# Two-block network on one Trainium2 core: the scores of parity 0 shifted by VectorE before one exponential, the steps of all queues reordered

## The reference

```python
xn = layernorm(x)
s = gru(xn)                      # a recurrence over 512 tokens, 256 hidden, as logs in the reference
g = silu(local_transformer(xn))  # 2 layers
x = x + s * g
xn = layernorm(x)
s = global_attention(xn)         # 16 heads over 512 tokens
g = silu(mixture_of_experts(xn)) # only the last item passes through the experts' real weights
x = x + s * g
```

```python
sim = einsum('bhwid,bhwjd->bhwij', bq, bk)
sim = where(mask, -finfo.max, sim)
attn = softmax(sim, axis=-1)
out = einsum('bhwij,bhwjd->bhwid', attn, bv)
```

## Time and profile before

| | us |
|---|---|
| median of 3 runs | 3660.54 (3658.41 to 3660.62) |
| profiled execution | 3663.09 |
| span of its instructions | 3661.3 |
| PE busy / DVE busy / ACT busy / POOL busy | 3026.1 / 2466.6 / 2551.7 / 922.2 |

### The profile page before, as it was taken

The page is one execution under the profiler, slowest core; times in us unless marked ns, Lnnn a source line. Parts: engine busy times, 40 slices in busy tenths (PEclk is TensorE's granted clock), DMA queues, the critical chain, the costliest instruction groups (busy, mean ns, idle before and its releaser), DMA issues.

```text
span 3661.3 us, 54935 instructions
## 1 busy us (share of the span) xinstructions
PE 3026.1 (83%) x20144; PEld 1454.9 (40%) x20144; DVE 2466.6 (67%) x4573; ACT 2551.7 (70%) x5722; POOL 922.2 (25%) x685
## 2 busy tenths in 40 slices
PE   4677897989888897979889897988889798988776
PEld 2343443434344343524344343534434343433242
DVE  3465867768685877768586776868586776857313
ACT  2466777868686777868677786868677786857444
POOL 1131323223131323313132322323132322312000
PEclk9889998999999999999999999999999998989887
DMA  2001010010101001010101001010101001011200
GB/s 71 3 1 51 18 51 17 14 58 19 58 14 51 21 31 41 14 58 18 54 18 51 21 25 47 14 58 19 54 18 47 21 14 55 19 51 36 83 9 16
DMA packets 113448, 122.78 MB, mean 34 GB/s; under 512 B 13426, under 2 KB 86684, under 8 KB 113180
## 3 DMA queue, kind: packets, MB, share of 16 engines
q1 hardware_dynamic: 113180, 119.26, 10.2%
HBM read 64.70 MB, written 54.53 MB: 33 GB/s over the span
## 4 chain that ended last, share of the span: by engine, by line
PE 45%; DVE 28%; ACT 19%; issue 5%; POOL 2%; SPq 1%; DMA 0%; DVEq 0%; POOLq 0%; ACTq 0%
PE pb L587 19%; PE o_bank L587 11%; PE s L587 6%; DVE nmax L1307 5%; PE e L587 5%; ACT ex L1033 5%; PE e L677 2%; DVE stat L1204 2%; ACT scratch L966 2%; DVE scratch L1213 2%; ACT mlp_h L990 1%; PE pb L731 1%; DVE scratch L1211 1%; DVE scratch L1245 1%; DVE stat L1233 1%
## 5 line engine op out<-in xcount | busy, mean ns | idle before, releaser
L1307 DVE TENSOR_REDUCE nmax<-s 128x1 f32<-128x512 f32 x1024 | 686.6, 684 | 404.1 <-PE s L587 398.3
L1033 ACT ACTIVATE ex<-s,nmax 128x512 f32<-128x512 f32 x1024 | 701.0, 686 | 253.0 <-DVE nmax L1307 218.9
L587 PE MATMUL o_bank<-ex,vsc 128*64 128x512 f32 x2048 | 542.0, 653 | 68.3 <-POOL vsc L1441 53.9
L587 PE MATMUL e<-wqkv,hsh 128*128 128x512 f32 x768 | 432.0, 645 | 85.4 <-ACT scratch L933 68.4
L1402 POOL TENSOR_TENSOR scratch<-scratch 128x1024 f32<-128x1024 f32 x128 | 304.6, 2379 | 768.8 <-DVE scratch L1214 599.7
L587 PE MATMUL s<-qs,ks 96*128 96x512 bf16 x1024 | 387.3, 404 | 121.1 <-ACT ex L1033 112.2
L1441 POOL TENSOR_TENSOR vsc<-vrow,rinv 128x256 f32<-128x256 f32 x256 | 167.6, 655 | 1114.6 <-DVE rinv L1315 770.4
L966 ACT ACTIVATE scratch<-pb,stat 128x128 f32<-128x128 f32 x1024 | 292.3, 375 | 88.6 <-DVE stat L1233 88.6
L1407 POOL TENSOR_TENSOR scratch<-scratch,stat 128x1024 f32<-128x1024 f32 x128 | 243.5, 1902 | 367.5 <-DVE stat L1226 367.5
L587 PEld LDWEIGHTS s<-qs,ks 96*128 96x128 bf16 x1024 | 92.2, 98 | 475.7 <-ACT ex L1033 239.3
L587 PEld LDWEIGHTS o_bank<-ex,vsc 128*64 128x64 f32 x2048 | 135.8, 145 | 341.1 <-issue 233.5
(11 more groups left out here) (196 smaller groups left out, 5746.5 us busy)
## 6 DMA issues: line engine op xcount, KB each, us to landing
parts_store<-side SPq DMA_DIRECT2D x64, 384.0 KB, 2.6
qs<-parts_store SPq DMA_DIRECT2D x128, 192.0 KB, 2.7
ks<-parts_store SPq DMA_DIRECT2D x128, 192.0 KB, 3.2
parts_store<-side SPq DMA_DIRECT2D x64, 256.0 KB, 3.0
parts_store<-side SPq DMA_DIRECT2D x64, 128.0 KB, 2.8
xin<-in_L_attn_x SPq DMA_DIRECT2D x16, 256.0 KB, 3.6
out<-o1T SPq DMA_DIRECT2D x16, 256.0 KB, 4.0
wqkv<-in_L_ffn_wqkv SPq DMA_DIRECT2D x1, 1536.0 KB
```

The lines of the kernel that those rows point to most:

```text
L587: return pe.matmul(o, l, r, start=start, stop=stop, skip_group_check=True)
L1033: A(ex[:, w % 2, j, :], s_bank[c % 2][:], ACT.Exp, bias=nmax[:, c % 8:c % 8 + 1], accum_out=rsum[:, w % 2, j:j + 1]).then_inc(GA, 1)
L1307: V.tensor_reduce(nmax[:, c % 8:c % 8 + 1], s_bank[c % 2][:], X, ALU.max, negate=True).then_inc(GV, 1)
```

## The change

For parity 0, VectorE now adds the negated maxima to the scores, all four heads in one instruction, with the maxima broadcast along the keys, and writes the sum to `prob[0]` in SBUF. ScalarE exponentiates those 128x512 values in place with one instruction. Parity 1 is as it was. VectorE's order in a score step is maximum of parity 0, sum of parity 0, maximum of parity 1. All four strings of `ORDER` are new as well; one is shown.

```diff
 ATTN_MARKS = {
-    "score": {"pe": ["s"], "dve": ["max0", "max1"]},
+    "score": {"pe": ["s"], "dve": ["max0", "sub0", "max1"]},
...
 ORDER = {
...
-    "pool": ("gpg2psgs2pgspgs2p2gpg2pgp2g3pgpgsgs3g"),
+    "pool": ("gpg2psgs2pgspgs2p3g3pgp2g3pgpgs3gsg"),
...
                 if kind == "prob":
-                    need(act, f, "dve", b, ("score", u // 2), f"max{u % 2}")
-                    sims, top = (bank_a, bank_b)[u % 2], stat[:, 64 + 4 * (u % 2):68 + 4 * (u % 2)]
-                    for r in range(PAIRS):
-                        last = A(prob[u % 2][:, r, :], sims[:, P * r:P * r + P], ACT.Exp, bias=top[:, r:r + 1])
-                    last.then_inc(FA, 1)
+                    if u % 2 == 0:
+                        need(act, f, "dve", b, ("score", u // 2), "sub0")
+                        A(prob[0], prob[0], ACT.Exp).then_inc(FA, 1)
+                    else:
+                        need(act, f, "dve", b, ("score", u // 2), "max1")
+                        for r in range(PAIRS):
+                            last = A(prob[1][:, r, :], bank_b[:, P * r:P * r + P], ACT.Exp, bias=stat[:, 68 + r:69 + r])
+                        last.then_inc(FA, 1)
...
                     V.tensor_reduce(top, sims, X, ALU.max, negate=True).then_inc(f.sem["dve"], 1)
+                    if par == 0:
+                        need(dve, f, "dve", b, s, f"max{par}")
+                        V.tensor_tensor(prob[par], sims, top.unsqueeze(2).broadcast_to([P, PAIRS, P]), ALU.add).then_inc(f.sem["dve"], 1)
```

More of the change, by code:

```diff
@@ L279 @@
 ORDER = {
[L280 to L286, removed]
-    "pool": ("gpg2psgs2pgspgs2p2gpg2pgp2g3pgpgsgs3g"),
+    "pe": ("4xsgpsgp7xgx2gp38xg2xsg3ps2gpxsp3xgpxspxq2gx2gpqgsgqpsprpgqps3gpqg2rgxp2grqrp2grq2rpq3gprgqpxgxqxgpr"
+           "grgqpgsgxrpqprgp3g2r2gpr2pqp2gpqsgrgqsgp2gprpqgxgspgsqspgrsrq2gprsprgsgrq2gqgsgprqgpr3gqgrs2gr2gqsrg"
+           "q3rsrsrsrgs5r2grgr15g"),
+    "act": ("xsp2gp2xgs2g2psp3xsgx2pg4p2gps2g2s3qgp2gq4p2gpq2gpgsxr2qgpq2g2pgsrqpg2qgspgqp2gqgp2qrp2gpgpgpgqp2grs"
+            "4p2gqpg2qgs2gqs2psp2g2pgsgqsgp2qr2s2pq3gpgprg3q2gpspgsgq4gqgsr2gq2s2qr2sgs2xs3r3srs3r17g"),
+    "dve": ("p3g5xs2g2p20x3g2s2psps2g2s3gqsgp2spgs2gp4xsgq2sr2g2pgrgp2grsrgrpgqgsrp2gr3gqrgsg2p2gr2gr2p2grpx3gqrs"
+            "g2psgr2g3xpgsgs2gq2gxr3pgrsrgsr3gpqs2g2s2grsgsgr3gqrgs3gxr2s2rs2r2sxrs2r2sg2s3r2gr7g"),
+    "pool": ("gpg2psgs2pgspgs2p3g3pgp2g3pgpgs3gsg"),
 }
```

## The result

The changed kernel takes 3695.16 us in the median of four runs (3691.91 to 3700.47), the kernel before 3660.58 beside it; the ratio is 1.0096, with a 95% interval of 1.0083 to 1.0109. That is +34.6 us. The forecast was +10.6 and the range ended at 3689, so the prediction was wrong, on the slow side.

A forecast was written before the change was run, and what follows sets the result against it. Bound taken as a chain of waits changing engines (45% TensorE, 28% VectorE, 19% ScalarE). VectorE places +1.7, ScalarE gains -1.0: +0.7 us a pass, times 15 = +10.6, forecast 3671 us; range 3646 to 3689.

The forecast's parts named there:

- What else the tables move: Steps passing one or two global steps in some forty places of a queue: counted as nothing.
- A3: Score step where the chain stays on VectorE to the end of line 1214: the sum costs +0.69 us a pass.
- B1: Score step with the chain over ScalarE's four exponentials: the single exponential gains 0.5 us a pass.
- B2: Score step near the MLP's last factor, with 1.89 us of idle time as cover: cost 0.
- A0: Score step followed by the GRU's sum after 0.28 us idle on VectorE: the sum delays it by 0.41 us.
- A1: Score step with VectorE idle 1.90 us ahead, into which a global row maximum moves: cost 0.
- A2: Score step with VectorE idle 1.58 us ahead, into which a global row maximum moves: cost 0.
- B3: Score step ahead of the copy that starts the output norm (line 1123): +0.57 us, taken as 0.6 a pass.
- B0: Score step, chain over ScalarE's exponentials; a global exponential fills 1.32 us idle, so waiting adds nothing: gain 0.5 us.
- VectorE as the bound: Rival: every new VectorE microsecond costs the average chain share; 3680 us, or 3698 without ScalarE's relief; chance 0.13.
- The clock: Rival: more TensorE idle time around A0 lengthens its slow-clock stretch, 2 us a pass; 3701 us; chance 0.05.
- Faster: Rival: TensorE's queue sets the pace at A3, so A3 costs nothing and B3 catches up; 3652 us; chance 0.26.

The follow-up runs named there:

- f4: Kernel before with only the new ORDER strings (four exponentials, no sum), plus 64 extra overwritten products a pass on TensorE: 3678.75 us, +46.1 on f1.
- e2: Kernel before with only the changed kernel's ORDER, four exponentials and no sum, no extra products: 3694.49 us, ratio 1.0094.
- j1: h1 with one more pair put back on GpSimd, rot0 of layer 0 ahead of the global scale_v8: 3654.62 us, ratio 0.9988.
- g4: f1 with only the stretch between score steps B1 and B2 in the new order: 3641.11 us, +8.4 on f1.
- j2: f1 with only one GpSimd pair exchanged, scale_v8 ahead of rot0: 3672.20 us, +39.5 on f1.
- g1: f1 with only the stretch around A3 in the new order on TensorE, ScalarE and VectorE: 3660.50 us, +27.8 on f1.
- f1: Kernel before with 64 extra bf16 128x512 products a pass in TensorE's gaps, results overwritten: 3632.66 us, ratio 0.9924.
- h3: f1 with only two pairs of neighbours exchanged in ScalarE's queue behind A3: 3634.29 us, +1.6 on f1.
- h1: f4 with the stretch around A3 put back to the old order on TensorE, ScalarE and VectorE, GpSimd left new: 3695.75 us, ratio 1.0101.
- w1: Kernel before with 54 extra overwritten bf16 128x512 products a pass in TensorE's gaps: 3632.7 us in a single run.

## Why the prediction was wrong

**The step that failed** is "What else the tables move ... I count as nothing: no step changes place with more than its neighbours". f4 shows that the moved steps alone cost 46 us, e2 34: all of the result. Most of it lies at two places: the stretch around A3 on TensorE, ScalarE and VectorE with GpSimd's pair (1.9 of 3.5 us a pass, f4 against j1, passes at the full clock), and the stretch from B1 to B2 (0.9, g4 and the table). j2 shows that even one exchange of neighbours can cost 39.5. The argument took the distance of a move for its price. It needed, for each exchange, what each of the two waits for and who waits for the second. The count was low too: written out, without the expert's steps, the two tables differ at 68 places (21 on TensorE, 29 on ScalarE, 16 on VectorE, 2 on GpSimd), where steps move by up to four positions, and not only past global steps. For the pair on GpSimd, as j2 has it in the old order, all of it stood in the trace of before, in the timeline above: rot0 ran from 1694.85, the reciprocal that scale_v8 needs ended at 1696.47, scale_v8 takes 0.62, so rot0 would start at 1697.1 and be 2.2 us late, and line 938 began 0.1 us after rot0's end. j2 measured 2.2. I read three queues of the table and the trace of two engines, and did not look at GpSimd, because it is busy a quarter of the time. In the changed kernel the pair's own share is small (above); the stretch on the other three engines costs 1.7 a pass by itself (g1, in the old order), and which of its exchanges do is not known.

**The prices of instructions** were right: 692 and 627 ns; VectorE +96.7 us for 88 forecast, ScalarE -59.8 for 67. TensorE's busy time was to stay and rose by 28.1 us with as many products; no run says why. The sum of the forecast has a slip of no weight (0.7 times 15 is 10.5).

**The sum's places**, at +0.7 a pass, were too dear for the new order, which gave +0.21 (the table above). Behind A0 the GRU's sum is 0.35 later (0.41 forecast), of which 0.21 is left at the next value step, and A1 gives it back. There VectorE went on without idle time, as foreseen:

```profile
1653.03 0.69 DVE L1239 TENSOR_TENSOR scratch<-pb,stat 128x512 f32<-128x512 f32 x1
1653.63 0.68 DVE L1236 TENSOR_REDUCE stat<-pb 128x4 f32<-128x512 f32 x1
1654.23 1.22 DVE L1170 TENSOR_TENSOR side<-side 128x1024 f32<-128x1024 f32 x1
```

A1 and A2 are hidden in the new order and not in the old one (+0.33, +0.78), which bears out the reason given, that a global maximum had gone into the idle time. B2 was to be hidden and cost 0.2 in both orders. A3 is where the table lost 2.1 and the sum only 0.15: with the queue late for another reason, the sum was not last; in the old order the sum cost 0.65 there for 0.69 forecast. B3 is +0.24 and not 0.6; in the old order it was 0.60.

**The gain at B0** did not come. ScalarE had to wait for the sum; of the timeline of after, for the first of the earlier trace rows:

```profile
1729.85 0.63 ACT L965 ACTIVATE scratch<-scratch 128x512 f32<-128x512 f32 x1 [0.98 <-DVE scratch L1239]
```

It had been idle 1.32 us there before; the global exponential took part of that and the sum the rest. At B1 0.39 of the 0.5 came, in the new order only; the old one had +0.56. From B0 to B2 the changed kernel is 0.4 us longer than before, where 1 us shorter was forecast (its lag goes from 1.15 to 1.53).

**The rivals.** VectorE as the bound (3680 to 3698) holds the measured time by accident: the chain's share on VectorE did not rise. The clock (3701) is not the difference either, as f1 to f4 show, though passes differ by it. "Faster" fell.

**Open.** Of the order's 46 us, the stretch around A3 with its pair is 24 (f4 - j1), B1 to B2 8 when put alone into the old order; some 14 are not placed by a run, of which the output norm's 0.37 a pass is 5.5. Which of the exchanges in TensorE's and ScalarE's queues around A3 make g1's 28 is known only by queue; two of ScalarE's are cleared by h3. What the pair is worth in the new order is an estimate.

## What to carry to other kernels

Where a change comes with a new instruction order, time the order apart from the code: here it was the whole result. For each exchange of neighbours in an in-order queue, compare when the operands of the two are there, and look for a consumer that starts the moment the second ends; do it for the least busy engine too, since one that is idle 75% of the time still holds what stands behind its queue's head. When undoing part of an order, take all engines' queues of that stretch together, or the rest makes a new mismatch (h1, j1: 41 us). And do not add prices of single exchanges: what each costs depends on what else is late there (39.5 and 27.8 apart, 24.1 together with the rest of the table).

## What the runs showed of the hardware beside that

- 64 products of bf16 128x512 a pass, put into TensorE's gaps, made the kernel before 0.76% faster: mean granted clock 0.979 for 0.937, 3632.7 us for 3660.6. The kernel before had 17.1 us a pass at the lower level (1.2 of 2.4 GHz), f1 none in most passes, although TensorE was busy 84 us more over the launch. The Trainium skill (TensorE: Matmul & The Clock Gate, A second HAM failure mode: psum-queue depth-cycling) says that short idle times between groups of products are enough to make the clock fall and rise again; the trace of before agrees as far as the clock falls at three fixed places a pass, ahead of which TensorE stood idle for part of the time (busy 1.37, 2.12 and 1.58 us of the last 4).
- Time at the lower clock does not cost the same everywhere: before, with 17.1 us of it, a pass was 2.5 us longer than one of w1 without any (208.2 against 205.7), 0.15 us for each, and somewhat more if the time of w1's own 54 products could be taken off; in w1 itself 3.4 us of it made a pass 1.2 to 1.6 longer, 0.4 for each. That it was cheap before because TensorE was waiting in much of it is argued from its low busy time there (4.24 us of 8).
